# Layer norm and the split of attention's weights placed inside the lora feed-forward, and two split key tiles of four in attention's product with the values

## The chip, the cores and the metric

The kernel runs on one core of a Trainium2 chip. The metric is the device time of one execution in microseconds (us). The engines are named as in the profile: PE (TensorE; PEld is its weight load), DVE (VectorE), ACT (ScalarE), POOL (GpSimd) and SP (SyncE, which here only issues DMAs).

## The reference

Two layers on 2048 tokens of width 256, float32. Layer 0 is a linear-attention block (time mix) and a feed-forward of lora experts; layer 1 is softmax attention with block-scaled weights and a routed expert feed-forward. Each block adds its result to the tokens and reads them through a layer norm. What the change touches:

```python
def _L0_ffn_ref(...):                      # E = 8 experts, 2 of them a token, F = 1024, R = 16
    base_h1 = x @ W1 + b1
    a = gelu_new(base_h1[:, None, :] + l1) # l1: the expert's own low-rank part
    ca = a * combine[:, :, None]
    mix = ca.sum(axis=1)
    out = mix @ W2 + combine.sum(-1, keepdims=True) * b2 + l2

def _L1_attn_ref(...):                     # 16 heads of 128, keys: all 2048 tokens
    def _mxfp4_matmul(x, codes, scales, block_size=32):
        w = codes * jnp.repeat(scales, block_size, axis=0)
        return x @ w
    q = _mxfp4_matmul(x, wq_codes, wq_scales) + bq      # k and v likewise
    scores = jnp.einsum('bqhd,bkhd->bhqk', q, k) / jnp.sqrt(jnp.float32(HEAD_DIM))
    attn = jax.nn.softmax(scores, axis=-1)
    out = jnp.einsum('bhqk,bkhd->bqhd', attn, v).reshape(B, S, NUM_HEADS * HEAD_DIM)
    return _mxfp4_matmul(out, wo_codes, wo_scales) + bo
```

## The kernel before

The tokens lie in `x_tok` as 16 tiles of 128 rows; a block is 512 tokens (4 tiles), and there are 4 blocks. The four stages stand one behind the other with barriers between, and inside a stage each engine has its own queue of instructions, written out by hand, with semaphores between the queues.

**Split pairs.** Many products are made from pairs: a float32 operand is written as `hi` (the value in the `fp32r` format, L1719 on ACT for probabilities) and `lo` (the rest, L1916 on POOL), and `three` (L917 to L919) adds hi x hi, hi x lo and lo x hi. A product of plain float32 operands is one instruction in the program and two records of PE in the trace.

**Layer norm before attention.** `layer_norm_tokens` is a stage of its own: DVE statistics, one square root on ACT, DVE normalises 16 tiles, PE transposes them, and ACT and DVE write `x_hi` and `x_lo`. Meanwhile SP loads q's and k's first weights and POOL splits them.

**Lora's main loop** (L1200 to L1300). For each block of tokens PE goes through 8 slices f of the hidden layer: `first(f+1)` (nine matmuls), `second(f)` (three, after the first of two gelus of slice f has read the same PSUM bank) and `down_rank(f-2)` (two plain products of 512 columns, four records). ACT makes two gelus a slice (L1270), DVE weighs them (L1285) and adds them into `lf_mix` (L1288). After the 8 slices come four output tiles of nine plain products each (L1256, L1260), which DVE adds to `x_tok` (L1300). POOL only adds a bias to the 16 token tiles (L1207, L1210), and SP is idle.

**Attention** (L1315 to L1980). The work is cut into 64 units (16 heads x 4 token blocks), each of 4 steps; a step scores 4 key tiles of 128 (12 matmuls into `at_psum_s`). ACT keeps the scores (L1706), DVE takes the running maximum (L1782) and subtracts it (L1771), ACT takes the exponent (L1712) five steps later, POOL sums the probabilities (L1941, L1946, L1950, L1955), and PE multiplies them with v (`weigh`) six steps after the scores. Of the four key tiles of a step one is a split pair and three are plain (`PAIRED = (1, 1, 1, 1)`); `p_hi` and `p_lo` have two slots. Steps also carry projections of q, k (4 steps in 16), v (7 steps in 32), the output projection and three sets of transposes. The weights of attention come as codes and scales: SP loads one DMA of codes and four of scales for each head or pair of heads, and POOL makes hi and lo in three operations (L1423, L1425, L1428) in chosen steps.

Of the kernel before, what the change touches and what calls it, by code (L numbers as in the profile page):

```python
# [51 lines left out]
class BlockNorm:  # L52


    def __init__(self, nc, ln, x_tok, x_hi, x_lo, ident, alloc, semaphore):
        self.nc, self.ln, self.x_tok, self.x_hi, self.x_lo, self.ident = nc, ln, x_tok, x_hi, x_lo, ident
        self.stats = alloc("bn_stats", [P, NT, 6], F32)
        self.mean_var = alloc("bn_mean_var", [P, NT, 2], F32)
        self.rstd = alloc("bn_rstd", [P, NT], F32)
        self.offset = alloc("bn_offset", [P, NT], F32)  # L60
        self.eps = alloc("bn_eps", [P, 1], F32)
        self.offset_ready = semaphore("bn_offset_ready")

    def begin(self):
        self.tiles, self.stds, self.copied = self.ln.before * NT, self.ln.std, self.ln.copied
        self.ln.before += 1
        self.ln.std += NB

# [22 lines left out]
    def normalise(self, act, b, rows):  # L91
        nc, ln = self.nc, self.ln
        act.wait_ge(self.offset_ready, b + 1)
# [5 lines left out]
    def turn(self, pe, b, rows, psum):  # L99
        nc, ln = self.nc, self.ln  # L100
        for j in range(TPB):
            pe.wait_ge(ln.norm_ready, self.tiles + b * TPB + j + 1)
            for c in range(NC):
                last = nc.tensor.transpose(psum[:, c, bass.ts(j, P)], rows[:, j, bass.ts(c, P)], self.ident[:])
        last.then_inc(ln.transposed, 1)

    def take_hi(self, act, b, psum):
        nc = self.nc
        act.wait_ge(self.ln.transposed, self.tiles + b + 1)
        for c in range(NC):  # L110
            nc.scalar.activation(self.x_hi[:, c, bass.ts(b, BT)], psum[:, c, :], ACT.Copy).then_inc(self.ln.hi_copied, 1)

    def take_lo(self, dve, b, psum):
        nc, tok = self.nc, bass.ts(b, BT)
        for c in range(NC):
            dve.wait_ge(self.ln.hi_copied, self.copied + NC * b + c + 1)
            nc.vector.tensor_tensor(self.x_lo[:, c, tok], psum[:, c, :], self.x_hi[:, c, tok].bitcast(F32),
# [804 lines left out]
def lora_ffn(nc, w, x_tok, ident, ln, x_hi, x_lo):  # L922
# [14 lines left out]
    with ExitStack() as ctx:  # L937
# [22 lines left out]
        with ExitStack() as stage:  # L960
# [8 lines left out]
            with ExitStack() as inner:  # L969
# [26 lines left out]
                def split_weights(pool):  # L996
# [5 lines left out]
                                  copy_split(nc, ln, x_hi, x_lo), loads, loaded, split_weights)  # L1002


            with ExitStack() as inner:
# [37 lines left out]
                with nc.Block() as block:  # L1043
                    @block.gpsimd
                    def _(pool):
                        pool.wait_ge(split_steps, 3)
# [128 lines left out]
        with ExitStack() as inner:  # L1175
# [17 lines left out]
            t2_psum = semaphore("lf_t2_psum")  # L1193
# [1442 lines left out]
```

## Time and profile before

| | us |
|---|---|
| median of the runs (2791.83 to 2798.86, three) | 2796.91 |
| the profiled execution, whole | 2791.96 |
| its span | 2790.1 |
| busy in the span: PE | 2665.0 (96%) |
| DVE | 2050.6 (73%) |
| POOL | 1827.0 (65%) |
| ACT | 1472.9 (53%) |

The profiled execution took 1.9 us more than its span. Busy times overlap; a matmul's duration overlaps the next one's, so how far apart two of them start says more than how long one took. Lora's main loop runs from 294 to 507 us, attention from 528 to about 2540.

### The profile page before, as it was taken

How to read it: one execution, taken by the hardware profiler on the slowest of the kernel's cores; microseconds unless marked ns; L12 is line 12 of the kernel's file. 1: busy time of each engine (PE TensorE's matmuls, PEld its weight loads, DVE VectorE, ACT ScalarE, POOL GpSimd, SP SyncE). 2: the span in 40 equal slices, each digit the busy share in tenths (PEclk: the TensorE clock that was granted, in tenths of full speed). 3: DMA queues.
4: the chain of work that ended last, by engine and by line, in shares of the span. 5: the costliest groups of instructions: out<-in, count | busy, mean ns of one | idle time of the engine just before them, and what ended most of it. 6: DMA issues, size and time to landing. Idle time of an engine off the chain costs nothing. (4 is left out here: it accounts for less than half of the span.)

```text
span 2790.1 us, 32396 instructions
## 1 busy us (share of the span) xinstructions
PE 2665.0 (96%) x10762; PEld 1825.2 (65%) x10763; DVE 2050.6 (73%) x3021; ACT 1472.9 (53%) x1837; POOL 1827.0 (65%) x1146
## 2 busy tenths in 40 slices
PE   7886999799999999999999999999999999997998
PEld 2333676567777677777767766776777677764765
DVE  6866434588888888888888888888888888886221
ACT  2323222266666665666666566656656665665122
POOL 2533400367877977787787779778877977785433
PEclk9998899899999999999999999999999999999999
DMA  2001000100000000000000000000000000004621
GB/s 67 0 0 53 0 0 0 39 13 5 16 1 14 12 9 10 7 18 1 14 12 8 7 8 20 1 14 4 16 1 14 8 4 5 1 1 87 233 60 48
DMA packets 58311, 57.90 MB, mean 21 GB/s; under 512 B 8910, under 2 KB 53201, under 8 KB 58162
## 3 DMA queue, kind: packets, MB, share of 16 engines
q1 hardware_dynamic: 55186, 48.79, 6.4%
q0 software_dynamic: 2976, 7.22, 0.9%
q8 instruction: 81, 1.33, 0.2%
q14 instruction: 68, 0.56, 0.1%
HBM read 46.65 MB, written 10.24 MB: 20 GB/s over the span
## 5 line engine op out<-in xcount | busy, mean ns | idle before, releaser
L1706 ACT ACTIVATE at_prob<-at_psum_s 128x1024 f32<-128x1024 f32 x512 | 520.7, 1017 | 642.5 <-PE at_psum_s L919 571.3
L1782 DVE TENSOR_TENSOR at_top<-at_psum_s,at_top 128x512 f32<-128x512 f32 x960 | 662.6, 690 | 169.2 <-ACT at_prob L1706 149.2
L1630 PE MATMUL at_psum_o<-at_prob,at_v 128*128 128x512 f32 x1536 | 703.5, 594 | 2.3 <-issue 1.4
L1771 DVE TENSOR_TENSOR at_prob<-at_prob,at_psum_m 128x1024 f32<-128x1024 f32 x512 | 603.4, 1210 | 0.4 <-PE at_psum_m L1618 0.4
L1946 POOL TENSOR_TENSOR at_acc<-at_acc,at_prob 128x1024 f32<-128x1024 f32 x189 | 449.0, 2376 | 195.6 <-ACT at_prob L1712 194.3
L1712 ACT ACTIVATE at_prob<-at_prob 128x1024 f32<-128x1024 f32 x512 | 536.9, 1049 | 24.3 <-DVE at_prob L1771 24.3
L1950 POOL TENSOR_TENSOR at_acc<-at_acc,at_prob 128x1024 f32<-128x1024 f32 x189 | 456.2, 2414 | 0.0
L1630 PEld LDWEIGHTS at_psum_o<-at_prob,at_v 128*128 128x128 f32 x1536 | 283.2, 190 | 262.1 <-issue 236.7
L917 PE MATMUL at_psum_s<-at_q_hi,sw_gate_up_hi 128*128 128x512 f32 x1024 | 402.4, 393 | 5.3 <-DVE sw_gate_up_lo L1763 5.3
L919 PE MATMUL at_psum_s<-at_q_hi,sw_gate_up_lo 128*128 128x512 f32 x1024 | 401.5, 392 | 0.0
L918 PE MATMUL at_psum_s<-at_q_lo,sw_gate_up_hi 128*128 128x512 f32 x1024 | 400.3, 391 | 0.0
L1916 POOL TENSOR_TENSOR at_p_lo<-at_prob,at_p_hi 128x512 fp32r<-128x512 f32 x256 | 331.8, 1296 | 0.6 <-ACT at_p_hi L1719 0.6
L1941 POOL TENSOR_TENSOR at_acc<-at_prob 128x1024 f32<-128x1024 f32 x63 | 151.1, 2398 | 206.5 <-ACT at_prob L1712 176.2
L919 PEld LDWEIGHTS at_psum_s<-at_q_hi,sw_gate_up_lo 128*128 128x128 f32 x1024 | 192.3, 188 | 43.6
L917 PEld LDWEIGHTS at_psum_s<-at_q_hi,sw_gate_up_hi 128*128 128x128 f32 x1024 | 192.4, 188 | 43.0 <-DVE sw_gate_up_lo L1763 6.6
L918 PEld LDWEIGHTS at_psum_s<-at_q_lo,sw_gate_up_hi 128*128 128x128 f32 x1024 | 192.4, 188 | 37.1
L917 PE MATMUL at_psum_o<-at_p_hi,at_v_hi 128*128 128x512 f32 x256 | 202.6, 792 | 0.7 <-POOL at_p_lo L1916 0.7
L1815 DVE SCALAR_TENSOR_TENSOR x_tok<-at_psum_w,at_rsum,x_tok 128x256 f32<-128x256 f32 x256 | 111.9, 479 | 102.4 <-PE at_psum_w L919 102.4
L1719 ACT ACTIVATE at_p_hi<-at_prob 128x512 fp32r<-128x512 f32 x256 | 161.5, 631 | 8.1
L1423 POOL TENSOR_TENSOR at_w_hi<-at_codes,at_scales 128x256 fp32r<-128x256 f32 x32 | 23.5, 735 | 196.4 <-DMA at_scales<-in_at_wq_scales 185.9
L1270 ACT ACTIVATE lf_hidden<-lf_psum_h,lf_b 128x512 f32<-128x512 f32 x64 | 40.9, 684 | 146.7 <-PE lf_psum_h L919 146.7
L917 PE MATMUL at_psum_w<-x_hi,at_w_hi 128*128 128x512 f32 x256 | 103.9, 406 | 4.2 <-PEq L158 4.2
(349 smaller groups left out, 4400.0 us busy)
## 6 DMA issues: line engine op xcount, KB each, us to landing
ef_gate_up<-in_ef_gate_up SPq DMA_DIRECT2D x8, 1024.0 KB, 14.2
ef_down<-in_ef_down SPq DMA_DIRECT2D x8, 512.0 KB, 14.1
ef_rows_in<-ef_zeros SPq DMA_DIRECT2D x23, 128.5 KB, 8.2
ef_rows<-ef_rows_in SPq DMA_DIRECT2D x23, 128.5 KB, 2.2
x_tok<-in_L_attn_x SPq DMA_DIRECT2D x4, 512.0 KB, 6.9
lf_w<-in_L_ffn_W SPq DMA_DIRECT2D x2, 1024.0 KB, 7.0
at_codes<-in_at_wq_codes SPq DMA_DIRECT2D x16, 128.0 KB, 2.1
at_scales<-in_at_wq_scales SPq DMA_DIRECT2D x64, 32.0 KB, 2.9
```

Of the source, the lines that this page charges most:

```text
L917: nc.tensor.matmul(out, a_hi, b_hi, start=start, stop=False, **kw)
L918: nc.tensor.matmul(out, a_hi, b_lo, start=False, stop=False, **kw)
L919: return nc.tensor.matmul(out, a_lo, b_hi, start=False, stop=stop, **kw)
L1630: nc.tensor.matmul(psum_o[:], v[:, plain_at[kt], half], prob[u % 2][:, kt, :], start=(c == 0 and t == PAIRED[c]), stop=False)
L1706: nc.scalar.activation(pair(u, c, half), psum_s[:, 2 * half:2 * half + 2, :], ACT.Copy).then_inc(kept, 1)
L1712: nc.scalar.activation(part, part, ACT.Exp, scale=SCALE).then_inc(exp_done, 1)
L1719: nc.scalar.activation(p_hi[:, n % 2, 0:PAIRED[c]], prob[u % 2][:, c * KPC:c * KPC + PAIRED[c], :], ACT.Copy).then_inc(p_hi_ready, 1)
L1771: nc.vector.tensor_tensor(part, part, psum_m[:].unsqueeze(1).to_broadcast([P, 2, BT]), ALU.subtract).then_inc(shifted, 1)
L1782: nc.vector.tensor_tensor(top[:, u % 2, :], psum_s[:, t, :], top[:, u % 2, :], ALU.max).then_inc(maxed, 1)
L1916: nc.gpsimd.tensor_tensor(p_lo[:, n % 2, 0:PAIRED[c]], part, p_hi[:, n % 2, 0:PAIRED[c]].bitcast(F32), ALU.subtract).then_inc(p_lo_ready, 1)
L1946: nc.gpsimd.tensor_tensor(acc2[:], acc2[:], pair(u, c, 0), ALU.add).then_inc(summed, 1)
L1950: nc.gpsimd.tensor_tensor(acc2[:], acc2[:], pair(u, c, 1), ALU.add).then_inc(summed, 1)
```

## The change

- **Layer norm.** The stage `layer_norm_tokens` ahead of attention goes. `BlockNorm`, which served only the norm after attention, is used twice. Lora's loop is written out for its four blocks, and in block b it normalises block b-1: DVE statistics in slice 0, ACT's square root in slice 1, DVE's inverse in 2, ACT's normalising into `t2` in 3, PE's 8 transposes into `psum_d` in 4, ACT's `x_hi` in 5 and DVE's `x_lo` in 6. The last block is normalised at the start of attention and transposed in its step 1.
- **Ring.** `hidden` has 4 slices instead of 8; a gelu then waits for `down_rank` and `mix` of four slices before. PE no longer waits at each block's end for DVE's last addition.
- **Weights.** The 32 pieces of attention's weights (8 each of q, k, v, o; 256 x 256 values) are loaded, multiplied by their scales (POOL, `make_whole`), copied to hi (ACT, `piece_part`), subtracted to lo (POOL, `piece_rest`) and stored in DRAM as hi and lo (0.5 MB), one piece for each slice of lora's loop, with two buffers. Attention then loads ready pairs, two DMAs instead of five, and POOL has no weights to split there.
- **Product with the values.** `PAIRED = (2, 2, 2, 2)`: two of the four key tiles of a step are split pairs, and the copies to `p_hi` and `p_lo` are of 1024 columns instead of 512. Key tiles of v follow suit.

```diff
-    PAIRED = (1, 1, 1, 1)
+    PAIRED = (2, 2, 2, 2)
...
+                @block.sync
+                def _(sp):
+                    def load_piece(p):
...
+                        sp.dma_start(whole[:, p % 2], codes.rearrange("(c p) n -> p c n", p=P)).then_inc(piece_loaded[p % 2], 16)
+                        sc = sc.rearrange("(c q) n -> q c n", q=NSC)
+                        for q in range(NSC):
+                            sp.dma_start(scales[q * BLK:(q + 1) * BLK, p % 2],
+                                         sc[q].partition_broadcast(BLK)).then_inc(piece_loaded[p % 2], 16)
...
+                    load_piece(0)
+                    load_piece(1)
+                    for p in range(len(PIECES)):
+                        sp.wait_ge(piece_lo, p + 1)
+                        store_piece(p)
+                        if p + 2 < len(PIECES):
+                            load_piece(p + 2)
...
+                    def make_whole(p):
+                        pool.wait_ge(piece_loaded[p % 2], N_LOADS * (p // 2 + 1))
+                        nc.gpsimd.tensor_tensor(whole[:, p % 2], whole[:, p % 2], scales[:, p % 2],
+                                                ALU.mult).then_inc(whole_ready, 1)
+
+                    def piece_rest(p):
+                        pool.wait_ge(piece_hi, p + 1)
...
+                    for p in range(len(PIECES)):
+                        if p % 2 == 0:
+                            add_bias(p // 2)
+                        make_whole(p)
+                        if p >= 1:
+                            piece_rest(p - 1)
...
+                    def piece_part(p):
+                        act.wait_ge(whole_ready, p + 1)
...
+                        nc.scalar.activation(pieces[:, p % 2, 0, :], whole[:, p % 2].rearrange("p c n -> p (c n)"),
+                                             ACT.Copy).then_inc(piece_hi, 1)
+
+                    for b in range(NB):
                         for f in range(NF):
...
+                            gelu(b, 0 if f == 0 else 2 * f - 1, f, 0)
+                            gelu(b, 2 * f + 2 if f + 1 < NF else 2 * NF - 1, f, 1)
+                            piece_part(b * NF + f)
...
         def load_qk(sp, m, h):
...
+            piece = split_weights["qk"[m]][h // 2].rearrange("p s (c n) -> p s c n", c=NC)
+            for part, to in enumerate((w_hi, w_lo)):
+                sp.dma_start(to[:, m].bitcast(F32), piece[:, part, :, bass.ts(h % 2, HD)]).then_inc(qk_loaded[m], 16)
```

POOL's queue in lora's loop, where `lf_bias` and `x_tok` are the bias of a token tile, `lf_whole` is `make_whole` and `lf_pieces` is `piece_rest`. Before:

```order
L1207 TENSOR_SCALAR lf_bias<-lf_b,lf_wsum 128x256
L1210 TENSOR_TENSOR x_tok<-x_tok,lf_bias 128x256 [waits lf_biased_rows]
L1207 TENSOR_SCALAR lf_bias<-lf_b,lf_wsum 128x256
L1210 TENSOR_TENSOR x_tok<-x_tok,lf_bias 128x256 [waits lf_biased_rows]
L1207 TENSOR_SCALAR lf_bias<-lf_b,lf_wsum 128x256 [waits lf_biased]
```

and in the changed kernel:

```order
L1265 TENSOR_TENSOR lf_whole<-lf_whole,lf_scales 128x512 [waits lf_piece0_loaded]
L1265 TENSOR_TENSOR lf_whole<-lf_whole,lf_scales 128x512 [waits lf_piece1_loaded]
L1272 TENSOR_TENSOR lf_pieces<-lf_whole,lf_pieces 128x512 [waits lf_piece_hi]
L1278 TENSOR_SCALAR lf_bias<-lf_b,lf_wsum 128x256
L1281 TENSOR_TENSOR x_tok<-x_tok,lf_bias 128x256 [waits lf_biased_rows]
L1265 TENSOR_TENSOR lf_whole<-lf_whole,lf_scales 128x512 [waits lf_piece0_loaded]
L1272 TENSOR_TENSOR lf_pieces<-lf_whole,lf_pieces 128x512 [waits lf_piece_hi]
L1265 TENSOR_TENSOR lf_whole<-lf_whole,lf_scales 128x512 [waits lf_piece1_loaded]
```

The rest of a piece stands behind the making of the next piece, which waits for that piece's load. SP's queue there was empty and now is, from the first piece on (codes and scales in, the split pair out):

```order
L1241 DMA lf_whole<-in_at_wq_codes 128x2x256
L1244 DMA lf_scales<-in_at_wq_scales 32x2x256 x4
L1241 DMA lf_whole<-in_at_wk_codes 128x2x256
L1244 DMA lf_scales<-in_at_wk_scales 32x2x256 x4
L1249 DMA at_wq_split<-lf_pieces 128x1024 [waits lf_piece_lo]
L1241 DMA lf_whole<-in_at_wv_codes 128x2x256
L1244 DMA lf_scales<-in_at_wv_scales 32x2x256 x4
L1249 DMA at_wk_split<-lf_pieces 128x1024 [waits lf_piece_lo]
```

Each store, and each load after the second, waits for a `piece_rest`. ACT's queue in lora's loop, once the ring is full, has the copy of a piece (L1361) after the two gelus of each slice (L1354), ahead of the next slice's:

```order
L1354 ACTIVATE lf_hidden<-lf_psum_h,lf_b 128x512 [waits lf_mixed,lf_ranked,lf_h_psum] x2
L1361 ACTIVATE lf_pieces<-lf_whole 128x512 [waits lf_piece0_stored,lf_whole_ready]
L1354 ACTIVATE lf_hidden<-lf_psum_h,lf_b 128x512 [waits lf_mixed,lf_ranked,lf_h_psum] x2
L1361 ACTIVATE lf_pieces<-lf_whole 128x512 [waits lf_piece1_stored,lf_whole_ready]
L1354 ACTIVATE lf_hidden<-lf_psum_h,lf_b 128x512 [waits lf_mixed,lf_ranked,lf_h_psum] x2
```

Before, only the gelus stood there. PE's queue at one step's product with the values (`at_psum_o`), before:

```order
L1630 MATMUL at_psum_o<-at_prob,at_v 128x512 [waits at_exp_done,at_w_free]
L1630 MATMUL at_psum_o<-at_prob,at_v 128x512 [waits at_exp_done] x2
L917 MATMUL at_psum_o<-at_p_hi,at_v_hi 128x512 [waits at_p_lo_ready]
L918 MATMUL at_psum_o<-at_p_lo,at_v_hi 128x512
L919 MATMUL at_psum_o<-at_p_hi,at_v_lo 128x512
```

and in the changed kernel:

```order
L1683 MATMUL at_psum_o<-at_prob,at_v 128x512 [waits at_exp_done,at_w_free]
L1683 MATMUL at_psum_o<-at_prob,at_v 128x512 [waits at_exp_done]
L930 MATMUL at_psum_o<-at_p_hi,at_v_hi 128x512 [waits at_p_lo_ready]
L931 MATMUL at_psum_o<-at_p_lo,at_v_hi 128x512
L932 MATMUL at_psum_o<-at_p_hi,at_v_lo 128x512
L930 MATMUL at_psum_o<-at_p_hi,at_v_hi 128x512
L931 MATMUL at_psum_o<-at_p_lo,at_v_hi 128x512
L932 MATMUL at_psum_o<-at_p_hi,at_v_lo 128x512
```

One plain product has become three of the pair kind.

## Rows read from the trace of the kernel before

**Rows 1.** Busy time of the engines in two stretches, with granted clock and DMA.
```profile
core 0: us, PE busy (x) PEld busy (x) DVE busy (x) ACT busy (x) POOL busy (x), PEclk, DMA share, GB/s
420.00:500.00 80.00, 78.91 (x300) 56.46 (x299) 29.84 (x47) 15.99 (x24) 0.00 (x0) 1.00 0.00 0
...
1000.00:1500.00 500.00, 499.61 (x2124) 355.37 (x2123) 421.09 (x588) 316.95 (x372) 398.38 (x234) 1.00 0.04 10
```

**Rows 2.** Timeline in attention, one step's product: start us, us, engine, line, op.
```profile
1509.25 0.19 PEld L1630 LDWEIGHTS at_psum_o<-at_prob,at_v 128*128 128x128 f32 x1 [0.24 <-issue]
1509.68 0.19 PEld L917 LDWEIGHTS at_psum_o<-at_p_hi,at_v_hi 128*128 128x128 f32 x1 [0.24 <-issue]
...
1510.34 0.39 PE L918 MATMUL at_psum_o<-at_p_lo,at_v_hi 128*128 128x512 f32 x1
...
1510.56 0.39 PE L919 MATMUL at_psum_o<-at_p_hi,at_v_lo 128*128 128x512 f32 x1
```

**Rows 3.** The page's costliest groups: busy us, mean ns of one | idle before.
```profile
L1630 PE MATMUL at_psum_o<-at_prob,at_v 128*128 128x512 f32 x1536 | 703.5, 594 | 2.3 <-issue 1.4
...
L1946 POOL TENSOR_TENSOR at_acc<-at_acc,at_prob 128x1024 f32<-128x1024 f32 x189 | 449.0, 2376 | 195.6 <-ACT at_prob L1712 194.3
...
L1950 POOL TENSOR_TENSOR at_acc<-at_acc,at_prob 128x1024 f32<-128x1024 f32 x189 | 456.2, 2414 | 0.0
...
L1916 POOL TENSOR_TENSOR at_p_lo<-at_prob,at_p_hi 128x512 fp32r<-128x512 f32 x256 | 331.8, 1296 | 0.6 <-ACT at_p_hi L1719 0.6
...
L1270 ACT ACTIVATE lf_hidden<-lf_psum_h,lf_b 128x512 f32<-128x512 f32 x64 | 40.9, 684 | 146.7 <-PE lf_psum_h L919 146.7
```

**Rows 4.** Timeline of PE in lora's main loop.
```profile
293.99 0.79 PE L917 MATMUL lf_psum_h<-x_hi,lf_w_hi 128*128 x1 [1.20 <-PEq L1043]
...
331.92 3.62 PE L1256 MATMUL lf_psum_d<-lf_w,lf_mix 128*128 128x256 f32 x16
...
348.73 0.49 PE L917 MATMUL lf_psum_h<-x_hi,lf_w_hi 128*128 x1 [1.11 <-DVE x_tok L1300]
...
506.04 0.60 PE L1260 MATMUL lf_psum_d<-lf_B2T,lf_t 128*128 128x256 f32 x2
```

**Rows 5.** Timeline of PE at the start of attention.
```profile
528.36 0.77 PE L917 MATMUL at_psum_w<-x_hi,at_w_hi 128*128 128x512 f32 x1 [4.23 <-PEq L158]
...
535.30 0.47 PE L917 MATMUL at_psum_s<-at_q_hi,sw_gate_up_hi 128*128 128x512 f32 x1 [1.66 <-DVE sw_gate_up_lo L1763]
```

**Rows 6.** Timeline of SP's queue, one load of v's weights.
```profile
1952.12 0.38 SPq L1405 DMA_DIRECT2D at_v_codes<-in_at_wv_codes  x1
1952.54 1.88 SPq L1409 DMA_DIRECT2D at_v_scales<-in_at_wv_scales  x4
```

**Rows 7.** The stretches around that load; the last two columns are DMA share and GB/s.
```profile
1956.50:1957.00 0.50, 0.50 (x4) 0.42 (x3) 0.50 (x2) 0.50 (x2) 0.50 (x1) 1.00 0.39 82
1957.00:1957.50 0.50, 0.50 (x6) 0.41 (x5) 0.50 (x1) 0.50 (x2) 0.50 (x1) 1.00 0.00 0
1952.00:1957.50 5.50, 5.50 (x28) 4.25 (x27) 4.54 (x7) 3.27 (x4) 5.50 (x4) 1.00 0.46 95
```

**Rows 8.** DMA issues: KB each, median us from issue to landing.
```profile
ef_rows_in<-ef_zeros SPq DMA_DIRECT2D x23, 128.5 KB, 8.2
...
at_v_scales<-in_at_wv_scales SPq DMA_DIRECT2D x32, 64.0 KB, 3.3
```

**Rows 9.** Instructions on the tile of v's codes: ns min/median/max.
```profile
L1425 POOL TENSOR_TENSOR at_v_codes<-at_v_codes,at_v_scales x8: 1275/1290/1297, 529.6 to 2192.4; 128x512 f32<-128x512 f32 x8
```

**Rows 10.** Timelines of POOL and DVE in lora, with POOL's bias work and without.
```profile
320.19 0.92 POOL L1207 TENSOR_SCALAR lf_bias<-lf_b,lf_wsum 128x256 f32<-128x256 f32 x1
...
322.02 1.88 POOL L1207 TENSOR_SCALAR lf_bias<-lf_b,lf_wsum 128x256 f32<-128x256 f32 x1
...
321.49 1.11 DVE L1288 TENSOR_TENSOR lf_mix<-lf_hidden 128x512 f32<-128x512 f32 x1
...
408.50 0.69 DVE L1288 TENSOR_TENSOR lf_mix<-lf_hidden 128x512 f32<-128x512 f32 x1
```

**Rows 11.** A stretch of the time mix with PE busy less than half.
```profile
200.00:205.00 5.00, 2.04 (x7) 0.98 (x6) 4.73 (x6) 1.91 (x2) 2.36 (x2) 1.00 0.00 0
```

More of the change, by code:

```diff
@@ L103, in turn @@
             for c in range(NC):
-                last = nc.tensor.transpose(psum[:, c, bass.ts(j, P)], rows[:, j, bass.ts(c, P)], self.ident[:])
+                last = nc.tensor.transpose(psum[c][:, bass.ts(j, P)], rows[:, j, bass.ts(c, P)], self.ident[:])
         last.then_inc(ln.transposed, 1)
@@ L1185, in lora_ffn @@
             bias = sb("lf_bias", [P, 2, D])
+            whole, scales = sb("lf_whole", [P, 2, NC, D]), sb("lf_scales", [P, 2, NC, D])
+            pieces = sb("lf_pieces", [P, 2, 2, NC * D], F32R)
             psum_h = ps("lf_psum_h", [P, 4, BT])
@@ L1201, in _ @@
                 @block.gpsimd
                 def _(pool):
-                    for i in range(NT):
+                    def make_whole(p):
[4 more added lines that the diff above has]
+                        pool.wait_ge(piece_hi, p + 1)
+                        if p >= 2:
+                            pool.wait_ge(piece_stored[p % 2], 16 * (p // 2))
+                        nc.gpsimd.tensor_tensor(pieces[:, p % 2, 1, :], whole[:, p % 2].rearrange("p c n -> p (c n)"),
+                                                pieces[:, p % 2, 0, :].bitcast(F32), ALU.subtract).then_inc(piece_lo, 1)
@@ L1205, in _, with add_bias @@
+                    def add_bias(i):
                         if i >= 2:
@@ L1247, in _ @@
                                 down_rank(f - 2)
+                            if b >= 1 and f == 4:
+                                pe.wait_ge(added, b * TPB)
+                                norm.turn(pe, b - 1, rows, turn_psum)
                         down_rank(NF - 2)
-                        down_rank(NF - 1).then_inc(t2_psum, 1)
+                        down_rank(NF - 1)
+                        if b >= 1:
+                            pe.wait_ge(ln.lo_copied, norm.copied + NC * b)
                         for i in range(TPB):
-                            if i >= 2:
+                            if b * TPB + i >= 2:
                                 pe.wait_ge(added, b * TPB + i - 1)
@@ L1278, in _ @@
                 @block.vector
                 def _(dve):
-                    with dve.Fori(0, NB) as b:
+                    for b in range(NB):
                         tok = bass.ts(b, BT)
@@ L1479, in attention @@
+            for part, to in enumerate((wo_hi, wo_lo)):
+                sp.dma_start(to[:].bitcast(F32), split_weights["o"][h // 2, :, part, bass.ts(h % 2, D)]).then_inc(o_loaded, 16)
+        loaded = semaphore("at_loaded")
         with ExitStack() as inner:
@@ L1490, in attention @@
             v_whole = sb("at_v_whole", [P, max(PAIRED), 2 * HD])
-            p_hi, p_lo = (sb(f"at_p_{part}", [P, 2, max(PAIRED), BT], F32R) for part in ("hi", "lo"))
+            p_hi, p_lo = (sb(f"at_p_{part}", [P, PAIR_ROOM, BT], F32R) for part in ("hi", "lo"))
             prob = [sb(f"at_prob{j}", [P, KT, BT]) for j in range(2)]
@@ L2093, in expert_ffn @@
             LAST = NB - 1
+            turn_psum = [psum_y[:, c, :] for c in range(NC)]
             def route_bank(b):
```

296 lines of the change are left out of this document (148 added, 148 removed).

## The prediction

> **What bounds the kernel now.** I read the stretches of the span first. In lora's main loop PE is busy 78.9 of 80 us, in attention 499.6 of 500 [rows 1]. So PE sets the time in both, and an edit counts by what it does to PE's work or by a wait that it puts in front of PE. In attention I then read the gaps between the starts of PE's weight loads and matmuls [rows 2]: a record of a plain product tile follows the one before after 0.43 us, a member of a split triple after 0.23. A plain tile leaves two records (1536 records for 768 tiles), hence 0.86; a split pair takes three, hence 0.69. POOL's costliest groups [rows 3] say what the wider split asks of it. In lora, the starts of PE's groups [rows 4] give 54.7 us from one token block to the next (first block, cold at its start) and, less the 1.1 of idle before the next, 15.7 for its four output tiles; from the first product to the end of the last are 212.7 us. Between that end (506.64) and attention's first score (535.30) lie 28.7 us [rows 4, 5] in which PE has 16 tiles of transposes and two projections; these are the layer norm, two barriers and the first weights.
>
> **Part 1, the product with the values: -40 us.** Four plain tiles a unit become split pairs, 64 x 4 = 256 times 0.86 - 0.69 = 0.17: 43.5 us off PE. What it loads elsewhere: POOL's p_lo grows from 1.30 to the 2.4 that its other ops of 1024 columns take [rows 3]. A unit then has seven sums and four p_lo of 2.4 and one op of 1.3: 27.7 us. PE's unit is scores 48 x 0.23 = 11.0, product 4 x 3.10 = 12.4, q projection 1.4, three sets of transposes 1.3 and output 1.4: 27.5, and with k (5.6 in one unit of four) and v (11 in one of eight) 30.3 on average. So POOL is a hair above PE in the units without k and v, and below on average: its lag is covered by the step that lies between exponent and product. The bounds are 43.5 (no wait) and 30 (0.2 us a unit and some at the joints); I take 40, nearer the first since the lag is paid back in each fourth unit. ACT's copy also doubles, by about 0.4 us four times a unit; ACT was busy 317 of 500 us [rows 1] and hides it. The weight splits leave POOL here (about 2 us a unit, not in the 27.7), and the loads of ready parts go out as soon as the last product with the old ones is done, 30 us and more ahead of need: nothing.
>
> **Part 2, the layer norm between the stages: -15 us.** Three quarters of it go into lora's blocks, beside the longer wait of part 3. What is left at the joint: about 0.9 us to the new stage, q's two parts issued 0.47 apart and landed 3.3 later [rows 6, 8]: 4.7. The six q and six k products with their copies took from 528.36 to 535.30 = 6.9 [rows 5], after which the first score can start: 11.6 instead of 28.7, so 17.1 less; the last block's norm now stands in step 1 (8 transposes, two copies, two subtractions), 2 us back. Bounds -12 and -17.
>
> **Part 3, splitting the weights in lora: +79 us.** This is the term that decides. There are 32 pieces, one after each slice f of the hidden layer, and ACT's copy of a piece stands in ACT's queue ahead of the next slice's gelus, on which PE's `second` waits. POOL makes whole(p+1) ahead of rest(p), and SP loads p+2 only after rest(p). So whole(p+2) needs load(p+2), which needs rest(p), which stands behind whole(p+1): two buffers, but one serial chain per piece,
> period P = load L + whole 1.3 + rest 1.3 + 0.1 of handing over, with 1.29 from the same shape in attention [rows 9].
> L: attention's v load has exactly these five DMAs and this size. It was issued from 1952.12, and its bytes flowed until 1957.0 [rows 6, 7]: 4.9. The five issues alone take 2.3, 0.47 each, and the last lands 3.3 after its issue [rows 8]. Ahead of it now goes the store of the piece before: 0.47 of issue, and 0.5 MB in the same queue. With bytes for nothing L = 5.4. The upper end is the 8.2 to landing behind a burst of stores [rows 8]. I take 6.0, near the lower end, since the v load kept the DMA engines busy for only 0.46 of 5.5 us [rows 7], and the store finds room there. P = 8.7, against PE's 4.6 a slice (37.9 / 8) [rows 4].
> A block: the copies of its first two pieces find their data ready, since PE's output tiles gave the chain time. The copy of piece 2 waits for copy 0.6, rest 1.3, load 6.0 and whole 1.3 = 9.2 after the first copy, and pieces 3 to 6 for P each: 9.2 + 34.8 = 44.0. From there to the block's last gelu and `down_rank`s 0.6 + 0.7 + 0.7 + 3 x 1.72 = 7.2, the output tiles 15.7 [rows 4], and until the next block's first copy two `first` of 2.07, a `second` of 0.7 and a gelu of 0.7 [rows 3] = 5.5. Together 72.4 (eight periods, 69.6, fit in). The stage: 8 to the first copy + 3 x 72.4 + 44.0 + 22.9 = 292, so 292 - 213 = +79. The bounds: L 5.4 gives P 8.1, block 69.4, stage 280, +67; L 8.2 gives P 10.9, where eight periods (87.2) set the block, stage 347, +135.
> The rest is free under that wait: bias adds (POOL waits for loads anyway), the norm's DVE and ACT ops, two table loads a block, the ring of four hidden slices; if the wait were not there, they would cost a few us. The barrier at each block's end, 1.1 us for PE [rows 4], goes too and is hidden now. PE, busy about half of such a loop, could lose its clock: a stretch at 2.04 of 5 us kept a granted clock of 1.00 [rows 11], so I put 0 and leave 10 in the range.
>
> **Sum.** 2791.96 (the profiled execution: span 2790.1 and 1.9 around it) + 79 - 15 - 40 = 2816. The median of the runs shown is 5 above that execution; I set 2819.
>
> **Rival A: the load is quicker than its neighbour, faster.** If five DMAs overlap down to their first latency (0.9 from issue to first bytes) and the 0.46 x 5.5 = 2.5 us of engine time [rows 7], L = 0.47 + 0.9 + 2.5 = 3.9, P 6.6, block 61.9, stage 250, +37: 2774. It decides below L = 4.8, where the stage costs the 55 that the other parts give. For it: the store's bytes could be free. Against: the very same load took 4.9 without a store, and SP issues one DMA per 0.47 us. [...] Chance 0.13.
> **Rival B: POOL binds attention too.** Its 27.7 against 27.5 us, plus handing over, leaves 25 instead of 40: 2834. For it: POOL's sums already run back to back within a step, with no idle time before L1950 [rows 3]. Against: the lag has a step to hide in. 0.10.
> **Rival C: POOL and DVE disturb each other.** A bias op took 0.92 us or 1.88, and DVE's mix 1.11 us beside POOL against 0.69 with POOL idle [rows 10]. If each piece carries one such 0.96, P = 9.7, eight periods set the block at 77.3, stage 311: 2835. The Trainium skill, "GPSIMD Engine Reference", section "Specifications", speaks against this change in the same way: POOL shares its SBUF interfaces with VectorE and contends with DVE ops that have two SBUF inputs, as all three DVE ops of a slice have; the rows agree. Against: DVE is busy only 2.1 of 8.7 us, and POOL's ops of 512 columns kept to 1.29 in attention. 0.07.
>
> **Numbers.** The forecast itself has 0.70, with 2799 to 2860 as its own range (L 5.4 to 7.3, the other parts at their bounds). Range 2786 to 2860: down into rival A, up over B and C. A measurement here tells 0.3% (8.4 us) from no change. Faster by more: most of A, 0.08. Within: the rest of A and the forecast's lowest end, 0.13. Slower: 0.79.
>
> **What would show it.** Right: in lora ACT's copy of a piece idle before it, released by POOL; POOL's whole idle, released by the scales' DMA; copies 8.7 us apart inside a block and about 72 from block to block; PE idle some 80 us there, released by ACT's gelu; a lora loop of some 290 us; the first score 12 us after it; attention's PE above 99% and a unit 0.6 us shorter. Wrong: copies less than 7.3 us apart, or PE idle before p_lo in attention.

## The result and the profile after

| | before | after |
|---|---|---|
| median of the runs, us | 2796.72 | 2881.55 (2880.08 to 2884.73) |
| ratio, 95% interval | | 1.0307 (1.0290 to 1.0325) |
| span of the profiled execution | 2790.1 | 2878.3 |
| lora's main loop, first product to last | 212.7 | 315.1 |
| from there to attention's first score | 28.7 | 10.7 |
| attention, first score to last product with v | 2003.4 | 2004.8 |

Slower by 3.1%, 85 us by the medians, where 22 were forecast; the time lies above the range. In front of lora's loop 3.4 us were lost, behind attention 1.1 gained, which is what these parts vary by from kernel to kernel below (its start lay between 291.9 and 297.4). So the +88 of the spans are lora's loop (+102), the joint (-18) and an attention in which **none of the 40 us showed**.

The stretches of after, by the view of [rows 1] (engines in the order PE, PEld, DVE, ACT, POOL, each busy us and count, then granted clock, DMA share, GB/s):

```profile
300.00:400.00 100.00, 78.14 (x269) 53.25 (x267) 36.57 (x53) 24.87 (x38) 37.87 (x31) 0.90 0.44 112
400.00:500.00 100.00, 72.48 (x248) 48.91 (x248) 30.33 (x49) 26.82 (x44) 35.57 (x32) 0.85 0.44 105
500.00:600.00 100.00, 76.79 (x245) 50.69 (x246) 34.25 (x54) 26.24 (x42) 36.43 (x32) 0.84 0.42 116
1000.00:1500.00 500.00, 491.40 (x2196) 367.38 (x2195) 430.72 (x581) 344.86 (x370) 442.32 (x194) 1.00 0.03 10
```

PE, busy 78.9 of 80 us in lora before, now stands a quarter of the time there. In attention it lost 8 of 500 us, where [rows 1] had 499.6. These 8 are small on any page, and over 2000 us they make 33, most of what the product missed.

**Lora.** Who waited for whom in the loop (297 to 613 us; engine, what it waited for, us in total, times, longest):

```profile
PE lf_psum_h L930 <- ACT lf_hidden L1354: 72.5, 17, 6.6
```
```profile
ACT lf_pieces L1361 <- POOL lf_whole L1265: 111.8, 24, 7.4
```
```profile
POOL lf_whole L1265 <- DMA lf_scales<-in_at_wk_scales: 53.1, 8, 8.2
POOL lf_whole L1265 <- DMA lf_scales<-in_at_wq_scales: 44.0, 8, 6.2
POOL lf_whole L1265 <- DMA lf_scales<-in_at_wo_scales: 42.5, 8, 5.6
POOL lf_whole L1265 <- DMA lf_scales<-in_at_wv_scales: 37.6, 8, 5.5
```

Read from the top it is the forecast's chain: PE waits for a gelu, which stands in ACT's queue behind the copy of a piece, which waits for the whole, which waits for the scales, 24 times of 32. Six copies of a block wait so; its first two find their data made. From one block's first copy to the next are 78.5 us on average (72.4 forecast).

**Attention.** PE's waits over 700 to 2500 us, before and then after:

```profile
PE at_psum_o L1630 <- issue: 1.4, 7, 0.2
PE at_psum_o L1630 <- DVE at_oT_lo L1803: 0.8, 1, 0.8
```
```profile
PE at_psum_m L1671 <- DVE at_row_top L1851: 15.7, 14, 1.2
PE at_psum_w L930 <- DVE at_q_lo L1824: 7.4, 7, 1.1
PE at_psum_o L1683 <- issue: 6.8, 7, 1.0
PE at_psum_o L930 <- POOL at_p_lo L1983: 1.1, 1, 1.1
```

The waits are 29 us longer. They lie in the units with v's projections and the one after: counted from first score to first score, a unit without k and v took 27.54 us where it had taken 28.25, as forecast, one with most of v's projections 38.39 where it had taken 35.75, and the one after it 30.34 where it had taken 29.64. Behind them stands **DVE**, not POOL, which the rivals had named. What grew in DVE's queue there (line, op, tiles, count, busy us and mean ns, idle before), before and after:

```profile
L1844 DVE TENSOR_TENSOR at_v_lo<-at_v_whole,at_v_hi 128x256 fp32r<-128x256 f32 x28 | 19.3, 688 | 1.0
L1841 DVE TENSOR_TENSOR at_v_hi<-at_psum_w,at_bv 128x256 fp32r<-128x256 f32 x28 | 11.6, 414 | 0.0
```
```profile
L1905 DVE TENSOR_TENSOR at_v_lo<-at_v_whole,at_v_hi 128x512 fp32r<-128x512 f32 x28 | 50.5, 1802 | 1.0
L1902 DVE TENSOR_TENSOR at_v_hi<-at_psum_w,at_bv 128x512 fp32r<-128x512 f32 x28 | 19.1, 681 | 0.0
```

Both ops have twice the columns. The one that reads PSUM and a bias takes 1.6 times as long; the one that reads two tiles of SBUF takes 2.6 times. A timeline of DVE and of POOL around one of them (start, us, engine, line, op) shows why:

```profile
1131.55 0.69 DVE L1901 TENSOR_TENSOR at_v_whole<-at_psum_w,at_bv 128x512 f32<-128x512 f32 x1
1132.15 0.68 DVE L1902 TENSOR_TENSOR at_v_hi<-at_psum_w,at_bv 128x512 fp32r<-128x512 f32 x1
1132.87 2.61 DVE L1905 TENSOR_TENSOR at_v_lo<-at_v_whole,at_v_hi 128x512 fp32r<-128x512 f32 x1
```
```profile
1132.55 2.39 POOL L2016 TENSOR_TENSOR at_acc<-at_acc,at_prob 128x1024 f32<-128x1024 f32 x1
```

POOL's op had begun 0.32 us earlier and ended at 1134.94; `at_v_lo` ended 0.54 later by these rounded rows, at 1135.48. It did not run slowly, it stood until POOL was through and then took its half microsecond. Of the 32 such ops of the kernel 29 began beside a POOL op with 0.40 to 2.06 us left, and each ended 0.55 us after it (0.56 once); the three that began with POOL idle took 0.69. The Trainium skill, "SBUF — State Buffer", section "Who interferes with whom", says just that: DVE and GpSimd share a pair of ports under an exclusive lock, which a DVE op with two SBUF inputs needs beside a GpSimd op that reads SBUF, and the second one blocks until the first has ended. This trace agrees. Per group of eight units (seven groups in 700 to 2500 us) all of DVE's ops on v took 10.5 us before and 15.5 after, 40 us more over the eight groups, about what PE's product saved.

### The profile page after: what moved, and what is told of

It reads as the page before. It is cut to its first block and busy times, and to the rows that moved or that the text cites. A ratio compares the mean times of both kernels' runs of the same rounds, so it can differ in the third digit from the quotient of the medians.

```text
span 2878.3 us, 32505 instructions
## 1 busy us (share of the span) xinstructions
PE 2659.3 (92%) x11018; PEld 1880.4 (65%) x11019; DVE 2086.4 (72%) x2979; ACT 1619.9 (56%) x1891; POOL 2064.1 (72%) x1042
## 3 DMA queue, kind: packets, MB, share of 16 engines
q1 hardware_dynamic: 74002, 82.34, 10.2%
## 5 line engine op out<-in xcount | busy, mean ns | idle before, releaser
L1983 POOL TENSOR_TENSOR at_p_lo<-at_prob,at_p_hi 128x1024 fp32r<-128x1024 f32 x256 | 616.1, 2407 | 1.2 <-ACT at_p_hi L1775 1.2
L1683 PE MATMUL at_psum_o<-at_prob,at_v 128*128 128x512 f32 x1024 | 483.0, 594 | 8.2 <-issue 6.8
L930 PE MATMUL at_psum_o<-at_p_hi,at_v_hi 128*128 128x512 f32 x512 | 298.8, 584 | 5.7 <-POOL at_p_lo L1983 5.7
L1683 PEld LDWEIGHTS at_psum_o<-at_prob,at_v 128*128 128x128 f32 x1024 | 185.5, 190 | 145.3 <-issue 125.6
L1775 ACT ACTIVATE at_p_hi<-at_prob 128x1024 fp32r<-128x1024 f32 x256 | 271.1, 1059 | 8.3 <-PE at_psum_o L932 0.2
L932 PE MATMUL at_psum_o<-at_p_hi,at_v_lo 128*128 128x512 f32 x512 | 202.2, 395 | 0.0
L931 PE MATMUL at_psum_o<-at_p_lo,at_v_hi 128*128 128x512 f32 x512 | 200.3, 391 | 0.0
L1265 POOL TENSOR_TENSOR lf_whole<-lf_whole,lf_scales 128x512 f32<-128x512 f32 x32 | 41.2, 1289 | 177.2 <-DMA lf_scales<-in_at_wk_scales 53.1
L1384 DVE TENSOR_TENSOR lf_hidden<-lf_hidden,lf_weights 128x512 f32<-128x512 f32 x64 | 51.0, 803 | 145.8 <-ACT lf_hidden L1354 145.6
```

Of the source, the lines that this page charges most:

```text
L930: nc.tensor.matmul(out, a_hi, b_hi, start=start, stop=False, **kw)
L931: nc.tensor.matmul(out, a_hi, b_lo, start=False, stop=False, **kw)
L932: return nc.tensor.matmul(out, a_lo, b_hi, start=False, stop=stop, **kw)
L1683: nc.tensor.matmul(psum_o[:], v[:, plain_at[kt], half], prob[u % 2][:, kt, :], start=(c == 0 and t == PAIRED[c]), stop=False)
L1775: nc.scalar.activation(p_hi[:, at:at + PAIRED[c], :], prob[u % 2][:, c * KPC:c * KPC + PAIRED[c], :], ACT.Copy).then_inc(p_hi_ready, 1)
L1983: nc.gpsimd.tensor_tensor(p_lo[:, at, :], part, p_hi[:, at, :].bitcast(F32), ALU.subtract).then_inc(p_lo_ready, 1)
```

## The experiments

Two theories and their rivals were open. For attention: **theory V** (the wider product saves PE what was forecast, and DVE's longer work on v, `at_v_lo` above all, gives it back), against **S** (something in attention's new surroundings costs 40 us whatever the pairs are) and **B** (POOL is too slow for the doubled `p_lo`). For lora: the serial chain, with the question what its load is made of. The times are medians; the kernel before ran beside them with 2794.05, 2796.26 and 2795.68 us in the three sets of runs.

### Single pairs again

```diff
-    PAIRED = (2, 2, 2, 2)
+    PAIRED = (1, 1, 1, 1)
```

> The changed kernel with one split pair in four key tiles again, as before; the layer norm and the weight pieces stay. Its attention, with pairs doubled, took 2004.9 us where the kernel before took 2003.4 and the forecast said 40 less. Theory V (DVE): the wider product does save its 43 us of PE, and DVE's longer work on the split values (at_v_lo of 128x512 took 1723 ns, at 128x256 before 655 ns) gives it back as waits of PE. Then with single pairs attention takes 2003 again and the time stays where it is: 2875 to 2888. Theory S (surroundings): something else in the new attention (ready weights loaded in parts, the missing splits on POOL) costs 40 us whatever the pairs are. Then taking the wide product away adds its 43: 2918 to 2930. Theory B (POOL too slow for four p_lo of 1024 columns) expects the same as V here.

Measured: 2875.44 us, ratio 1.0291 (1.0273 to 1.0308), attention 2007.4. Taking the wider product away costs nothing. The time is 6 us lower, all of it in front of attention, where the edit changes nothing: the loop took 310.8 us here and 310.7 to 315.8 in the other kernels with the same loop and the same order of DMAs, so differences of some 5 us between medians can lie there, and attention's own time says more. S falls. The new surroundings do cost 4 us (2007.4 against 2003.4 before). DVE's work has its old size again (0.658 us for `at_v_lo`), and PE's waits of 700 to 2500 us are down to one row:

```profile
PE at_psum_o L1683 <- issue: 1.4, 7, 0.2
```

### A shorter v_lo

```diff
-  nc.vector.tensor_tensor(whole, psum[:, 0:len(paired), :], offset, ALU.add).then_inc(v_steps, 1)
+  nc.vector.tensor_copy(whole[:, 0:1, 0:1], psum[:, 0:1, 0:1]).then_inc(v_steps, 1)
...
-  made = nc.vector.tensor_tensor(v_lo[:, at, :], whole, v_hi[:, at, :].bitcast(F32), ALU.subtract)
+  made = nc.vector.tensor_tensor(v_lo[:, at, :], psum[:, 0:len(paired), :], v_hi[:, at, :].bitcast(F32), ALU.subtract)
```

> The changed kernel with less of DVE's work on the split values: at_v_lo is the PSUM tile less at_v_hi, and at_v_whole is not made (one element is copied in its place), so the bias of the values is left out of at_v_lo. Per split job DVE does about 1.4 us instead of 3.1, 6.6 us less per eight units. Theory V: PE's idle time in the units with v projections goes and the saving of the wide product shows: attention 1962 to 1972, the time 2840 to 2850. Theory S and theory B (POOL): DVE's queue is not what PE waits for, at most 5 us: 2874 to 2882.

This kernel leaves the values' bias out of `at_v_lo`. Measured: 2841.73 us, ratio 1.0165 (1.0147 to 1.0182), 39.8 below the changed kernel; attention 1971.9, which is 32.9 less. V stands and B falls: POOL had the same work as in the changed kernel, and PE waited for it once.

```profile
PE at_psum_o L930 <- POOL at_p_lo L1983: 0.8, 1, 0.8
```

That is PE's whole list of waits from 700 to 2500 us. Against single pairs in the same surroundings attention is 35.5 us shorter: this is the size of the wider product. In the 63 units before the last it gives 40.1 us; from the last unit's first score to the last product with v, where no further scores run beside it, it costs 4.6 (63.3 against 58.7).

### V split in PSUM, the arithmetic whole

```diff
-  whole = v_whole[:, 0:len(paired), :]
+  whole = psum[:, 0:len(paired), :]
...
-  nc.vector.tensor_tensor(v_hi[:, at, :], psum[:, 0:len(paired), :], offset,
-                          ALU.add).then_inc(v_steps, 1)
+  dve.wait_ge(v_steps, m + 1)
+  nc.vector.tensor_copy(v_hi[:, at, :], whole).then_inc(v_steps, 1)
```

> The changed kernel with the same arithmetic on the split values in another place: the projected values get their bias in place in PSUM, at_v_hi is a copy from there, and at_v_lo is PSUM less at_v_hi, so that none of the three DVE ops has two SBUF operands and at_v_whole is gone. Theory V: at_v_lo of 128x512 falls from 1723 ns (0.69 where POOL is idle, up to 2.61 where one of POOL's ops of 2.4 us runs) to 0.69, DVE does 2.1 us per split job instead of 3.1 and none of it waits for POOL, and nearly all of what the short form gave (39.8 us, with 0.7 less DVE work per job) is had: attention 1968 to 1980, the time 2838 to 2853. Rival: what the short form gave came mostly from the op left out, not from the second SBUF operand: 2858 to 2870.

Measured: 2853.19 us, ratio 1.0213 (1.0198 to 1.0229), 28.4 below the changed kernel; attention 1982.2, 22.7 less, 2 us outside what was expected of it and on V's side.

```profile
L1905 DVE TENSOR_TENSOR at_v_lo<-at_psum_w,at_v_hi 128x512 fp32r<-128x512 f32 x28 | 19.4, 691 | 1.0
```
```profile
PE at_psum_o L1683 <- issue: 5.7, 7, 0.8
PE at_psum_m L1671 <- DVE at_row_top L1851: 1.1, 7, 0.2
```

The number of ops and of columns is the same, and the biased values stand in PSUM instead of SBUF (so `at_v_hi` is a copy from there and waits for them). `at_v_lo` fell from 1.80 to 0.69 us and never waited for POOL. It ran through beside POOL's ops:

```profile
1120.64 0.69 DVE L1905 TENSOR_TENSOR at_v_lo<-at_psum_w,at_v_hi 128x512 fp32r<-128x512 f32 x1
```
```profile
1120.18 2.38 POOL L2016 TENSOR_TENSOR at_acc<-at_acc,at_prob 128x1024 f32<-128x1024 f32 x1
```

So of the 32.9 us that the short form gave in attention, 22.7 were the second SBUF operand; the other 10.2 are the 0.7 us an op that the short form also left out. These are 22 us of DVE's time over 32 ops, of which half reached PE.

### p_lo in two halves

```diff
-  nc.gpsimd.tensor_tensor(p_lo[:, at, :], part, p_hi[:, at, :].bitcast(F32), ALU.subtract).then_inc(p_lo_ready, 1)
+  for t in range(PAIRED[c]):
+      one = slice(at.start + t, at.start + t + 1)
+      last = nc.gpsimd.tensor_tensor(p_lo[:, one, :], part[:, t:t + 1, :], p_hi[:, one, :].bitcast(F32),
+                                     ALU.subtract)
+  last.then_inc(p_lo_ready, 1)
```

> The changed kernel with POOL's at_p_lo of 1024 columns made by two ops of 512 (1.3 us each). It tells how POOL holds DVE's at_v_lo up. Theory of a lock: a DVE op with two SBUF operands stands still until POOL's running op ends, then takes its 0.6: the op of 128x512 took up to 2.61 us beside a POOL op of 2.4. With p_lo in halves, those that fall on p_lo wait 1.3 at most, those on the sums of 2.4 as before: mean 1.72 falls to 1.3 to 1.6, and the time by 3 to 15 us: 2866 to 2878. Theory of shared bandwidth: DVE runs slowly as long as any POOL op runs, the mean stays at 1.7 and the time at 2880 to 2885, since POOL has a little more to do.

Measured: 2893.31 us, ratio 1.0356 (1.0341 to 1.0372), 11.8 **above** the changed kernel, and attention 2023.8, 19 more; the mean of `at_v_lo` rose from 1.72 to 1.87. Both expectations missed. The timelines show that the halves are not what `at_v_lo` mostly met: from the second group on, in both kernels, three of a group's four ran into one of POOL's sums, and only one into `p_lo`.

```profile
1128.19 2.56 POOL L1985 TENSOR_TENSOR at_p_lo<-at_prob,at_p_hi 128x512 fp32r<-128x512 f32 x2
1130.69 2.40 POOL L2020 TENSOR_TENSOR at_acc<-at_acc,at_prob 128x1024 f32<-128x1024 f32 x1
```
```profile
1130.74 2.90 DVE L1905 TENSOR_TENSOR at_v_lo<-at_v_whole,at_v_hi 128x512 fp32r<-128x512 f32 x1
```

It came 0.05 us behind the start of a sum of 2.40 and waited for all of that, then took 0.55: the lock again (POOL's end 1133.09, DVE's 1133.64). Which POOL op it meets is set by the schedule, the same from group to group, and the schedule had shifted by a few tenths. And POOL, with 0.19 us more to do per step, is now waited for:

```profile
PE at_psum_m L1671 <- DVE at_row_top L1851: 16.8, 14, 1.4
...
PE at_psum_o L930 <- POOL at_p_lo L1985: 5.8, 14, 0.6
```

So B was false by a narrow margin. The units tell how the 19 us divide. Two in every eight, in which no product of v is split and only POOL has more to do, took 28.05 and 28.42 us instead of 27.54 and 27.71: 9.6 us over attention. The units with v's projections and the ones after lost 6.6, where the longer stand of `at_v_lo` and POOL's pace can't be told apart, and the last unit 2.4.

### The rest ahead of the next whole

```diff
-                        make_whole(p)
                         if p >= 1:
                             piece_rest(p - 1)
+                        make_whole(p)
```

> The changed kernel with one edit in lora's loop: POOL makes at_pieces' rest of piece p before the whole of piece p+1, so that the load of p+2 is sent one POOL op and one load wait earlier and two loads are under way. Chain theory: the period of 9.1 us is L 7.0 + two POOL ops of 1.3 in one serial chain; with two loads under way it falls to (7.0 + 1.3 + 0.7 + 1.3)/2 = 5.2 or a little over, near PE's 4.6 to 5.3, the lora loop takes 225 to 245 us instead of 315 and the whole 2791 to 2811. Rival (the DMAs are bound by their queue or their bytes: a second load under way only makes each one longer): copies stay over 7.5 us apart, loop over 285, time over 2850. Second rival (clock): the loop gets its order back but PE's granted clock stays at 0.85 and the loop is 260 or more: 2825 or more.

Measured: 2811.92 us, ratio 1.0063 (1.0043 to 1.0082), 69.6 below the changed kernel; the loop 247.9 instead of 315.1, copies 3.7 to 6.7 apart inside a block. Two lines in another order undo four fifths of the kernel's loss and two thirds of the loop's: the period was a serial chain, and neither the DMAs' bytes nor the clock were its bound. The granted clock came back by itself (0.95 over the loop, where it was 0.87), with PE's waits for the gelu down from 72.5 us to 22.7 and the longest from 6.6 to 3.7. The loop and the time each came out a little above what was expected.

### The load ahead of the store

```diff
-                        store_piece(p)
                         if p + 2 < len(PIECES):
                             load_piece(p + 2)
+                        store_piece(p)
```

> The changed kernel with SP's two orders swapped: the load of piece p+2 goes ahead of the store of piece p. It tells how much of the 7.0 us from the end of one rest to the data of the next load is the store's. If it is the issue slot alone (0.35 to 0.47 us) the 28 waited periods of the loop give 10 to 13 us: 2868 to 2872. If the store's 0.5 MB is in the way of the load's bytes as well (another 0.5 to 1.2 us a period), 25 to 45 us: 2836 to 2857. If the load waits for something else, such as its own four broadcast DMAs one after another, no more than the slot.

Measured: 2856.14 us, ratio 1.0216 (1.0197 to 1.0235), 25.4 below. From the end of a rest to the whole two pieces later, averaged over the 30 pairs, 5.3 us instead of 6.7. So the store had 1.4 us of the load, of which its issue is 0.40 (372.60 to 373.00 in the rows of the next experiment); the other 1.0 is put down to its bytes, as was expected if they are in the way. The load without a store took 5.3 to 6.9 for the pieces of q, k and v and 4.0 to 5.0 for those of the output projection.

### Scales by two DMAs

```diff
-            N_LOADS = 16 * (1 + NSC)
+            N_LOADS = 16 * (1 + NC)
...
-  for q in range(NSC):
-      sp.dma_start(scales[q * BLK:(q + 1) * BLK, p % 2], sc[q].partition_broadcast(BLK))...
+  for c in range(NC):
+      sp.dma_start(scales[:, p % 2, c, :], sc[:, c].unsqueeze(1).to_broadcast([NSC, BLK, D]))...
```

> The changed kernel with the scales of a piece brought by two DMAs of all 128 partitions instead of four of 32, the same bytes; the load has three DMAs instead of five. The rest stays, the serial chain too. Load with the store ahead: 6.9 us from the end of one rest to the next whole on average. Issue theory (SP sends one DMA in 0.47 us and the last one's landing counts): 0.94 us less in each of the 28 waited periods, 26 us, 2850 to 2858. Bytes theory (the same bytes by the same queue take the same time): under 8 us, 2874 or more.

Measured: 2882.81 us, ratio 1.0316 (1.0300 to 1.0332): nothing. SP's queue in the changed kernel and here:

```profile
372.60 0.35 SPq L1249 DMA_DIRECT2D at_wo_split<-lf_pieces  x1
373.00 0.43 SPq L1241 DMA_DIRECT2D lf_whole<-in_at_wk_codes  x1
373.47 2.21 SPq L1244 DMA_DIRECT2D lf_scales<-in_at_wk_scales  x4
```
```profile
374.60 0.34 SPq L1249 DMA_DIRECT2D at_wo_split<-lf_pieces  x1
374.99 0.44 SPq L1241 DMA_DIRECT2D lf_whole<-in_at_wk_codes  x1
375.48 1.36 SPq L1244 DMA_DIRECT2D lf_scales<-in_at_wk_scales  x2
```

From the store's issue to the end of the last one SP needs 2.24 instead of 3.08 us, and on average the data comes no sooner (6.9 us from rest to whole, 6.7 before). The issue theory, which the forecast had leaned on too, is not borne out: 26 us were expected of it. But the average hides two changes. From rest to whole the pieces of q and k took 7.2 and 7.0 us where they had taken 7.5 and 7.4, those of v 6.9 (6.7), and those of the output projection 6.6 (5.3). The edit changed the pace of the bytes too, and so is no clean test of the issue alone. The DMA engines of the changed kernel over 370 to 385 us, in 40 slices of 0.375, show a load of k's:

```profile
DMA  0000000008999797911237125442000000000000
GB/s 0 0 0 0 0 0 0 0 0 339 415 404 224 197 314 238 98 25 36 87 74 41 25 87 76 44 57 60 0 0 0 0 0 0 0 0 0 0 0 0
```

Store and codes (0.75 MB) pass in seven slices at 197 to 415 GB/s; the 256 KB of scales, each row of 1 KB copied to 32 partitions, then trickle in at 25 to 98 for another 4.5 us. That copying alone does not make them slow. The output projection's scales are copied to 32 partitions by four DMAs just so, and land sooner (KB each, median us from issue to landing; k's 4.0, v's 3.5):

```profile
lf_scales<-in_at_wq_scales SPq DMA_DIRECT2D x32, 64.0 KB, 4.2
...
lf_scales<-in_at_wo_scales SPq DMA_DIRECT2D x32, 64.0 KB, 2.6
```

A load of an output piece in the changed kernel (394 to 404 us, slices of 0.25) and with two DMAs (395.5 to 403 us, slices of 0.1875):

```profile
GB/s 0 0 0 0 0 0 0 115 393 442 344 442 147 213 123 360 389 353 316 86 213 189 45 21 4 0 0 0 0 0 0 0 0 0 0 0 0 0 0 377
```
```profile
GB/s 0 0 0 0 0 0 0 153 459 393 393 350 437 262 262 87 126 268 393 382 251 98 93 98 93 76 87 93 98 93 93 104 93 98 93 49 16 0 0 0
```

By four DMAs these scales are through some 2 us after the codes; by two they flow at 76 to 104 GB/s for 3 us. What differs between the pieces in the program is that the output projection's rows stand one behind another in DRAM and those of q, k and v are cut out of rows of 2048 values; no run changed that alone, and why the bytes are slow stays open.

### Both repairs, and what beats both kernels

First the lora loop alone, with the scales of piece p+2 sent as soon as whole p is made, the codes after the rest, the store last:

```diff
                     for p in range(len(PIECES)):
+                        if p + 2 < len(PIECES):
+                            sp.wait_ge(whole_ready, p + 1)
+                            load_piece(p + 2, (1,))
                         sp.wait_ge(piece_lo, p + 1)
+                        if p + 2 < len(PIECES):
+                            load_piece(p + 2, (0,))
                         store_piece(p)
-                        if p + 2 < len(PIECES):
-                            load_piece(p + 2)
```

(with the rest first as above; part 1 are the scales, part 0 the codes).

> The changed kernel with the order of the rest ahead of the next whole, as in the run before (2811.9 us, loop 247.9, copies 5.5 apart, PE idle for ACT's gelu 22.7), and SP's work cut in three: the scales of piece p+2 as soon as whole p is made, the codes after rest p, and the store of p last. Chain theory: the wait of POOL's whole for scales goes, no copy waits, PE's 22.7 us go: loop 222 to 230, time 2786 to 2796. Rival (what is left comes from the added work on ACT, DVE and POOL, such as DVE ops that POOL holds up): only the waits on scales change place, under 10 us: 2802 or more.

Measured: 2803.49 us, ratio 1.0025 (1.0016 to 1.0035), the loop 237.9: 8.4 gained where 16 to 26 were expected. POOL's waits for scales are gone but for one at the start; PE still waits 16.2 us for ACT's gelu. The rival was nearer, and what it calls added work is looked for in the rows below. Together with v's split in PSUM:

> The two edits together, the values split in PSUM and the lora loop with rest first, scales early and the store last: 2881.6 less about 37 in attention and less 85 to 95 in lora's loop, 2746 to 2762, which is 1.2 to 1.8% faster than before. If the two gains share a cause or a resource (POOL or DMA), less: over 2765.

Measured: 2780.48 us, ratio **0.9942** (0.9928 to 0.9956), faster than before by 0.6% and than the changed kernel by 3.5%. The two gains add up to 106.5 (28.4 + 78.1) and 101.1 were had; the expectation, 2746 to 2762, had taken both too high. Loop 240.1, attention 1982.1. What is left in the loop:

```profile
300.00:530.00 230.00, 213.72 (x791) 150.00 (x791) 134.00 (x158) 76.06 (x122) 128.37 (x94) 0.96 0.49 144
```
```profile
366.21 1.28 ACT L93 ACT_TABLE_LOAD   x1
...
367.82 1.28 ACT L1358 ACT_TABLE_LOAD   x1
369.12 0.69 ACT L1358 ACTIVATE lf_hidden<-lf_psum_h,lf_b 128x512 f32<-128x512 f32 x1
```

The square root of the layer norm brings two table loads into ACT's queue, and PE stands 3.7 us for the gelu behind them, once in each of three blocks: 11 of the 16.2. And POOL's ops are longer than in the slow chain: `lf_whole` takes 1.66 us on average, there it took 1.29. That this is DVE's two-operand ops beside it fits what attention showed; no run here separates it.

> The two repairs together (values split in PSUM; rest first, scales early, store last), and the scales by two DMAs. There the chain no longer waits for loads on PE's path except at the start, so the same edit that gives 26 us in the serial chain gives 0 to 5 here: 2774 to 2782 against the 2780.5 without it. If loads still held the loop back, 10 or more.

Measured: 2780.24 us, ratio 0.9945 (0.9931 to 0.9958), as without the edit and as expected.

## Why the prediction was wrong

**Which way** it went, and why, was right: lora's chain decides, and its path is the one written down, from SP's load to PE's gelu. **How far** was wrong by 63 us (2881.55 against 2819), and the time lay above the range.

- **The product, -40: the step that failed.** PE's side was right. A unit without k and v gave 0.71 us where 4 x 0.17 = 0.68 was worked out, and the short form against single pairs gave 40.1 in the units before the last; the 4.6 that the last unit loses were not in the sum, and 35.5 are left. What failed is the list of what the wider split loads elsewhere. It had POOL's `p_lo` and ACT's copy and not DVE's three ops on v, which the same constant widens from 256 to 512 columns. DVE's work on v was in no term, rival or bound, and it took 33 us back (2004.8 against 1971.9), all of it in the units with v's projections (38.39 against 35.03) and the ones after (30.34 against 28.95). In [rows 1] DVE is busy 421 of 500 us; with 5 us more per eight units it was 431, and nothing in such an average says that the 5 lie in a few steps ahead of the maximum for which PE waits.
- **Lora, +79: mechanism right, size too small; 102.** By the parts: L was set at 6.0 and measured 6.7 (7.5 and 7.4 for q and k, 5.3 for the output projection). Without the store it was 5.3 where 4.9 had been read, and the store added 1.4 where 0.5 of issue and 0.6 of bytes were allowed. So a block's first copy and its seventh stood 47.6 us apart, where the working had 44.0: in four blocks 14 us. The second part is **the clock, set at 0**: PE stood 4.6 us before 432.07, and then the last slice ran at half rate (columns as in the first rows of this part).

```profile
430.00:431.00 1.00, 0.00 (x0) 0.00 (x0) 0.00 (x0) 0.19 (x1) 1.00 (x2) 0.50 0.00 0
...
435.00:436.00 1.00, 1.00 (x2) 0.34 (x1) 0.86 (x2) 0.00 (x0) 0.00 (x0) 0.50 0.74 214
436.00:437.00 1.00, 1.00 (x3) 0.52 (x2) 0.00 (x0) 0.00 (x0) 0.00 (x0) 0.65 0.46 138
437.00:438.00 1.00, 1.00 (x3) 0.39 (x3) 0.00 (x0) 0.00 (x0) 0.62 (x1) 1.00 0.00 0
```

  The granted clock was 0.50 (1.2 GHz) from 430 to 436 and 1.00 (2.4 GHz) from 437. Inside the chain this is free; from a block's seventh copy to its output tiles it isn't: 9.4 us (430.81 to 440.25) where 7.2 were worked out, 9.1 to 9.9 in the four blocks, 9 us in all. With the rest first three of the four stretches ran at 1.00 and took the 7.2; one of them:

```profile
398.74:405.95 7.21, 5.95 (x16) 2.95 (x17) 5.52 (x7) 2.52 (x4) 5.95 (x5) 1.00 0.70 203
```

  The stretch of [rows 11] was the wrong neighbour: PE was half idle there too, and kept 1.00. With the first copy a microsecond sooner than the 8 worked out, the two parts make the 23 that the term was short.
- **The joint, -15: 18.0** measured, a little past the bound of 17.
- **The free items** of the lora part: hidden under the wait, as put. Their price without it was put too low at "a few us": with the chain's wait gone the loop still takes 25 to 27 us more than before (237.9 and 240.1 against 212.7), and the table loads alone are 11 of them.
- **Rival A** (a quick load) fell: L was 6.7. The store was not free, and the 4.9 of [rows 6, 7] came back as 5.3 to 6.9 without a store for the pieces of q, k and v (4.0 to 5.0 for the output projection's). The reason given for the 4.9, one DMA per 0.47 us, is not borne out: with 0.84 us less of issue the load was as long. **Rival B** (POOL) was false in the changed kernel; with 0.19 us more a step POOL costs 9.6 us in the units without v. **Rival C** (POOL and DVE disturb each other) was real but looked for in the wrong stage. In lora's chain POOL's ops kept to 1.29 and 1.33; in attention it took DVE's `at_v_lo`.
- Of what should have been seen, the releasers, the chain and the joint came as written. The copies of pieces 2 to 6 of a block came 9.3 us apart, not 8.7; PE idle 72.5, not 80; attention's PE at 98.3%, not above 99.
- **Slips in the working** that decide nothing: 37.9 / 8 is 4.7, not 4.6; 8 x 9.7 is 77.6, not 77.3; 2816 and the 5 that the median is above the profiled execution make 2821, not 2819; rivals A and C count from 2816 and B from 2819.

## What to carry to other kernels

List every op that a constant sizes, on every engine, before costing it: here one tuple widened ops on four engines and three were counted. A DVE op that reads two SBUF tiles beside a busy POOL costs its own time plus what is left of POOL's op, so making POOL's ops longer makes such DVE ops longer; an operand kept in PSUM avoids it. With two buffers, release the one before filling the other on the same engine, or the two are one serial chain. PE's product may be worth its number and still give nothing, if the engine behind it has its work in the same few steps.

## What the runs showed of the hardware

- DVE's op with two SBUF operands ended 0.55 us (0.56 once) after the POOL op that ran at its start, at 512 columns, whatever was left of that op: 29 of 32 ops in the changed kernel, up to 2.61 us long, and 29 of 32 with p_lo in halves, up to 2.90. With POOL idle it took 0.69, and with one operand in PSUM 0.69, though 29 of the 32 had a POOL op beside them. It is a stand, not a slower pace.
- The same 256 KB of scales, by the same four DMAs of 32 partitions, landed 4.2 us after issue (median of q's) or 2.6 (the output projection's), behind the same 0.5 MB of store. Two DMAs of 128 partitions made q's and k's loads 0.3 to 0.4 us shorter and the output projection's 1.3 longer.
- The granted clock was at 0.50 when PE, after 4.6 us of standing, took up a slice's work, and from the copy of a block's seventh piece to its output tiles 9.4 us went by, where at 1.00 it was 7.2.
- A square root between gelus put two table loads of 1.28 us each into ACT's queue, and PE stood 3.7 us for the gelu behind them.
